# A graph network's edge loop on one core: counts moved ahead of the later sources, spans read at the body's head, ranks restarted behind each block's loop

## The reference, cut to what matters

```python
# layer 0: a two-layer message network, summed over the edges of each source
m = jnp.concatenate([x[row], x[col]], axis=1)
m = jax.nn.relu(m @ Wm1 + bm1)
m = jax.nn.relu(m @ Wm2 + bm2)
m_sum = jax.ops.segment_sum(m, row, num_segments=x.shape[0])

# layer 2: each source keeps only its first 10 edges, by rank in the list
rank = jnp.arange(E) - starts[row_s]
keep = (rank < NUM_NEIGHBORS).astype(x.dtype)

# layer 3: edge weights, summed over equal (source, target)
msg = edge_weight[:, None] * x[src]
agg = jax.ops.segment_sum(msg, dst, num_segments=N)
```

## Time and profile before

| what | value |
|---|---|
| median of three executions | 982.04 us (979.52 to 982.39) |
| profiled execution, span | 979.5 us; the page gives no other time of its own, and it lies at the lowest of the three |
| PE busy | 888.5 us, 91% of the span |
| DVE busy | 665.4 us, 68% |
| ACT busy | 502.9 us, 51% |
| POOL busy | 292.3 us, 30% |
| chain that ended last | PE 76%, DVE 13%, ACT 5%, issue 3% |
| mean granted clock of PE | 0.986 of full speed |

### The profile page before, as it was taken

The page is one execution under the profiler, slowest core; times in us unless marked ns, Lnnn a source line. Parts: engine busy times, 40 slices in busy tenths (PEclk is TensorE's granted clock), DMA queues, the critical chain, the costliest instruction groups (busy, mean ns, idle before and its releaser), DMA issues.

```text
span 979.5 us, 18566 instructions
## 1 busy us (share of the span) xinstructions
PE 888.5 (91%) x5440; PEld 549.7 (56%) x5474; DVE 665.4 (68%) x1778; ACT 502.9 (51%) x1009; POOL 292.3 (30%) x424
## 2 busy tenths in 40 slices
PE   3999968999899989999999989889998998899898
PEld 1556736878787878787887855522233222322244
DVE  6399995676667666667666674676858776877561
ACT  6232103555555555565555563746755665566621
POOL 5030027444444545455444510021132210112000
PEclk9999987999999999999999999999999999999999
DMA  3020022111111111112111200000000000000120
GB/s 82 19 91 1 1 78 97 52 54 53 60 49 65 44 64 43 65 48 70 37 64 41 51 33 1 1 0 1 1 1 1 0 1 1 0 1 1 69 104 22
DMA packets 19145, 35.87 MB, mean 37 GB/s; under 512 B 5280, under 2 KB 11552, under 8 KB 18976
## 3 DMA queue, kind: packets, MB, share of 16 engines
q0 software_dynamic: 7104, 19.41, 6.7%
q1 hardware_dynamic: 12000, 15.95, 4.6%
HBM read 29.56 MB, written 5.79 MB: 36 GB/s over the span
## 4 chain that ended last, share of the span: by engine, by line
PE 76%; DVE 13%; ACT 5%; issue 3%; DMA 1%; POOL 1%; DVEq 0%; ACTq 0%; POOLq 0%
PE PS L1396 9%; PE PS L1258 7%; PE PS L1252 6%; PE PS L1381 5%; PE PS L1177 5%; PE PS L1178 5%; PE PS L1192 5%; PE PS L1127 5%; PE PS L1387 4%; PE PS L1249 3%; PE PS L1299 3%; DVE OHd L988 3%; PE PS L1170 3%; PE PS L1350 2%; PE PS L1183 2%
## 5 line engine op out<-in xcount | busy, mean ns | idle before, releaser
L399 POOL DMA_INDIRECT BT<-Qtab,gidx x148 | 150.4, 1016 | 96.3 <-DVE gidx L815 61.1
L546 ACT ACTIVATE OHe<-OHs,sew 128x128 bf16<-128x128 bf16 x408 | 126.6, 389 | 61.9 <-PE PS L1258 61.4
L413 POOL TENSOR_SCALAR KV<-BT,pid 128x256 bf16<-128x256 uint8 x74 | 69.9, 945 | 174.2 <-DVE MS L890 168.1
L988 DVE CUSTOM_DVE_ANT_0 OHd<-PS,n1T 128x1024 bf16<-128x1024 f32 x96 | 112.1, 1219 | 9.5 <-PE PS L1350 9.5
L557 ACT ACTIVATE m2s<-m2s 128x512 f32<-128x512 f32 x68 | 42.9, 630 | 107.9 <-DVE m2s L916 107.9
L930 DVE TENSOR_SCALAR OHd<-iotaN,dstf 128x1024 bf16<-128x1024 f16 x136 | 63.6, 507 | 37.0 <-PE PS L1258 37.0
L916 DVE TENSOR_TENSOR m2s<-PS,bm 128x512 f32<-128x512 f32 x68 | 46.9, 690 | 53.9 <-PE PS L1178 53.9
L1177 PE MATMUL PS<-Wm,m1T 128*128 128x256 f32 x276 | 83.2, 383 | 0.0
L1178 PE MATMUL PS<-Wm,m1T 128*128 128x256 f32 x276 | 82.6, 381 | 0.0
L1258 PE MATMUL PS<-OHs,m2s 128*128 128x128 f32 x544 | 79.5, 290 | 0.1
L452 POOL TENSOR_TENSOR zl<-AL,Sx 128x8 f32<-128x8 f32 x12 | 2.6, 216 | 257.0 <-DVE Sx L988 257.0
(11 more groups left out here) (350 smaller groups left out, 1723.9 us busy)
## 6 DMA issues: line engine op xcount, KB each, us to landing
BT<-Wtab SPq DMA_DIRECT2D x1, 4096.0 KB, 13.9
BT<-Qtab,gidx POOLq DMA_INDIRECT x148, 2.8
BT<-Stab SPq DMA_DIRECT2D x1, 2048.0 KB, 10.5
Wtab<-H SPq DMA_DIRECT2D x4, 512.0 KB, 2.9
Wtab<-cs SPq DMA_DIRECT2D x4, 512.0 KB, 3.0
Qtab<-BT SPq DMA_DIRECT2D x1, 1024.0 KB, 4.5
Wn<-in_L_gnn_Wn SPq DMA_DIRECT2D x1, 1024.0 KB, 5.4
x<-in_x SPq DMA_DIRECT2D x1, 512.0 KB, 4.1
```

Source lines behind the costliest of these rows:

```text
L399: g.indirect_dma_start(out=G[:, p % SLOTS, k, :], out_offset=None, in_=Qtab, in_offset=bass.IndirectOffsetOnAxis(ap=gidx[:, p, k:k + 1], a ...
L546: a.activation(OHe[:, k, j, :], OHs[:, k, :], ACT.Copy, scale=sew[:, j, bass.ds(2 * g + k, 1)])
L988: v.tensor_tensor_reduce(junk[n % 2], bank(4, 2), mask[:, i, :], 1.0, 2 * FAR, ALU.subtract, ALU.max, Sx[:, i, hd:hd + 1]).then_inc(S("gat ...
```

## The change

PE's body is put in another order: the span is read at the head, before R'; C follows R'; and S follows C. The semaphore `counts_added` is now raised by S's first product, where M's first product raised it before. On DVE the source one-hots `OHs` come ahead of the message. At a block's end ACT copies the message sums ahead of the weights; PE restarts the ranks as soon as the message sums are out, the restart clearing bank 4 itself, and then clears banks 0 to 3 only. Behind the last block neither is done.

```diff
@@ ScalarE, at a block's end
                 eng.wait_ge(S("ranks_done"), end + 1)
+                a.activation(msum[:, :, b * P:(b + 1) * P], bank(4)[:, 0:F2].rearrange("p (f n) -> p f n", f=2),
+                             ACT.Copy)\
+                    .then_inc(S("msum_out"), 1)
                 if b >= 2:
                     eng.wait_ge(S(f"spilled{b % 2}"), 16 * (b // 2))
                 a.activation(TT[b % 2], bank(2, 2), ACT.Copy).then_inc(S("weights_out"), 1)
-                a.activation(msum[:, :, b * P:(b + 1) * P], ...
@@ VectorE, in the body
-                    message(g + 2)
-
                     eng.wait_ge(S("ranks_added"), g + 1)
                     eng.wait_ge(S("scaled_ready"), g + 1)
                     eng.wait_ge(S("counts_ready"), g + 1)
...
                     last.then_inc(S("src_onehots"), 1)
+                    message(g + 2)
                     eng.wait_ge(S("counts_added"), g + 2)
@@ TensorE
-            def ranks(pairs):
+            def ranks(pairs, anew=False):
-                for region, tri, k in pairs:
+                for i, (region, tri, k) in enumerate(pairs):
                     last = t.matmul(bank(4)[:, F2 + region * P:F2 + (region + 1) * P], tri[:], OHs[:, k, :],
-                                    start=False, stop=False, skip_group_check=True)
+                                    start=anew and i == 0, stop=False, skip_group_check=True)
                 return last
+            def restarted():
+                ranks(((0, beforeb, 0), (1, onesb, 0), (1, beforeb, 1)), anew=True).then_inc(S("ranks_restarted"), 1)
-            def sources(slot, blk):
+            def sources(slot, blk, behind=None):
                 for k in range(2):
                     for j in range(3):
+                        if behind is not None and k == 0 and j == 1:
+                            last.then_inc(behind, 1)
                         last = t.matmul(bank(5)[:, k * F2:(k + 1) * F2],
...
-            for b in range(NB):
-                eng.wait_ge(S("src_onehots"), g0 + 1)
-                ranks(((0, beforeb, 0), (1, onesb, 0), (1, beforeb, 1))).then_inc(S("ranks_restarted"), 1)
+            eng.wait_ge(S("src_onehots"), 1)
+            restarted()
+            for b in range(NB):
                 with eng.Fori(g0, end) as g:
+                    eng.wait_ge(S("spans"), 1)
+                    span = eng.value_load(rngi[0:1, bass.ds(g, 1)], min_val=1, max_val=NB * NB * NB - 1)
+                    first, least, past = eng.snap((span >> 6) & (NB - 1)), eng.snap((span >> 3) & 7), eng.snap((span & 7) + 1)
                     eng.wait_ge(S("ranks_read"), g + 1)
                     ranks(((0, notbefb, 0), (0, onesb, 1), (1, notbefb, 1))).then_inc(S("ranks_added"), 1)
-                    eng.wait_ge(S("spans"), 1)
-                    span = eng.value_load(rngi[0:1, bass.ds(g, 1)], min_val=1, max_val=NB * NB * NB - 1)
-
-                    eng.wait_ge(S("turned_onehots"), g + 3)
-                    sources((g + 2) & (SLOTS - 1), (span >> 6) & (NB - 1))
 
                     eng.wait_ge(S("scaled_ready"), g + 1)
                     eng.wait_ge(S("counts_ready"), g + 1)
-                    with eng.Fori((span >> 3) & 7, (span & 7) + 1, 2) as d:
+                    with eng.Fori(least, past, 2) as d:
...
+                    eng.wait_ge(S("turned_onehots"), g + 3)
+                    sources((g + 2) & (SLOTS - 1), first, S("counts_added"))
+
                     eng.wait_ge(S("m2_ready"), g + 1)
...
-                            if f == 0 and k == 0:
-                                last.then_inc(S("counts_added"), 1)
                     last.then_inc(S("pair_done"), 1)
@@ TensorE, at a block's end
+                eng.wait_ge(S("msum_out"), b + 1)
+                if b + 1 < NB:
+                    restarted()
+                eng.wait_ge(S("weights_out"), b + 1)
                 eng.wait_ge(S("counts_out"), b + 1)
-                eng.wait_ge(S("msum_out"), b + 1)
-                for k in range(5):
-                    t.matmul(bank(k), zeros[:, 0:P], zeros[:, 0:BANK], start=True, stop=True)
+                if b + 1 < NB:
+                    for k in range(4):
+                        t.matmul(bank(k), zeros[:, 0:P], zeros[:, 0:BANK], start=True, stop=True)
```

More of the change, by code:

```diff
@@ L566, in _ @@
                 a.activation(TT[b % 2], bank(2, 2), ACT.Copy).then_inc(S("weights_out"), 1)
-                a.activation(msum[:, :, b * P:(b + 1) * P], bank(4)[:, 0:F2].rearrange("p (f n) -> p f n", f=2),
-                             ACT.Copy)\
-                    .then_inc(S("msum_out"), 1)
                 g0, end = end, after
```

## The result

The changed kernel takes 1036.3 us (four runs, 1034.47 to 1036.87) against 982.2 us before: ratio 1.0554, 95% interval 1.0538 to 1.057. The forecast was 1024 with a range of 1003 to 1034. The direction was right, the size 12 us short and 2 us outside the range. The profiled execution has a span of 1032.7 us against 979.5, so 53.2 us more, where the sum of the prediction had 43.7.

The account below looks back on a forecast made before the run. A loop through DVE and PE's sequencer was to bound each pair: 60 pairs x 0.64 = 38.4, seven block ends 4.7, one more pair 0.6, together 43.7 us on 982.0, 1025.7, put 2 lower at 1024; range 1003 to 1034.

Parts of the forecast that it names:

- S's steps behind C: Inside a pair on PE: S's six address steps stand uncovered behind C's loop, 0.62 us, making C to S 1.74 us.
- DVE's ring: Inside a pair: S, message, `OHd`, `prod`, `OHc`, C, next S; 6.14 us, taken as 6.12, 0.64 more a pair.
- `OHd` to `prod` 301.44 - 300.59 = 0.85: On DVE inside a pair: time from the start of `OHd` to `prod`, put at 0.85 us.
- The other five terms: S to message 1.18, message to next operation 0.61, `prod` to `OHc` end 1.16, on to C 0.60, to S 1.74 us.
- steps hidden by C: On PE behind C: S's steps may be partly hidden by C's last products, so the forecast was put 2 us lower.
- The second ring through the transposes: Inside a pair: L's transposes wait for the message about 0.1 us more, which was said to lie within the DVE loop.
- The block ends: At seven block ends: 9.80 us against 9.13, 0.67 more each, although 1.04 us of exposed span reading goes.
- the clock as a rival: With PE idle in each pair the granted clock might fall oftener; ten pairs at about 1.3 us, 1037 us; chance 0.04.
- Inside a block it was covered before and still is, by L: nothing: Inside a block, moving the span's reading to the head was said to change nothing, since L covers it either way.
- The sequencer hides it (960): C's products are queued far ahead, so S's steps pass beside C and 0.22 us a pair goes; 960 us, chance 0.09.
- PE alone (1009): PE's own steps set the pair at 5.88 us, 0.40 more, the DVE loop being shorter; 1009 us, chance 0.10.
- the cancelling case (981): S's steps are hidden by half and block ends gain 1.04 us, so gains and loss cancel; 981 us, chance 0.05.

Follow-up runs that it names:

- Experiment 2: The changed kernel with five of S's six address steps done at the body's head and kept in registers; 1009.7 us, 1.0208 of the kernel before.
- Experiment 3: The changed kernel with GpSimd's one-hots held back until the counting one-hots `OHc` are there; 1038.2 us, 1.0504 of the kernel before.
- experiment 6: The changed kernel with the four clearing products at a block's end done three times over; 1032.7 us, 1.0461 of the kernel before.
- experiment 9: The changed kernel with the span read behind R' again, before C's set-up; 1045.1 us, 1.0572 of the kernel before.
- experiment 4: The kernel before with only the span's reading moved to the head of PE's body, ahead of R'; 947.9 us, 0.9591.
- experiments 1: The changed kernel with S ahead of C again: with DVE's order as before 952.5 us, 0.9636; with DVE's new order 947.8 us, 0.961.
- experiment 10: The changed kernel with S's address steps kept in registers and GpSimd's one-hots held back, together; 1067.4 us, 1.0794 of the kernel before.
- experiment 8: A second span reading added: in the kernel before, between R' and S, 1035.0 us, 1.0475; with the reading at the head, there, 968.2 us, 0.9781.

## Why the prediction was right in kind and short in size

*S's steps behind C: right.* 1.74 us from C to S, as worked out. Experiment 2 took five steps away and the distance fell by 0.48. The sequencer's records of L1197 in one pair of the changed kernel:

```profile
L1197 PEldq FUSED_REGOPS  x5: 46/46/65, 228.7 to 229.3; - x5
L1197 PEldq ALU_OP  x3: 32/36/36, 228.5 to 228.8; - x3
```

They last 0.03 to 0.05 us each and begin at 228.5, with S at 228.99. Start to start is what counts, 0.6 us and not 0.2. The Trainium skill (Perfetto Trace Analysis, Per-engine timelines) says that for an instruction of the sequencer only the execution is reported, and the runs agree.

*DVE's ring sets the pair: right, with one term too small.* This is the step that failed: "`OHd` to `prod` 301.44 - 300.59 = 0.85". It measures 1.02. The other five terms are within 0.01. The 0.85 was read where only the last 0.25 us of GpSimd's one-hot lay beside `OHd`:

```profile
299.90 0.94 POOL L413 TENSOR_SCALAR KV<-BT,pid 128x256 bf16<-128x256 uint8 x1 [2.07 <-DVE MS L890]
```

In the changed kernel `OHd` follows the message at once, and so does GpSimd's one-hot, which waits for that same message. The two kernels' lines over the whole trace (ns min/median/max), first of before:

```profile
L930 DVE TENSOR_SCALAR OHd<-iotaN,dstf x136: 467/485/658, 163.3 to 563.7; 128x1024 bf16<-128x1024 f16 x136
...
L413 POOL TENSOR_SCALAR KV<-BT,pid x74: 910/945/962, 145.7 to 562.5; 128x256 bf16<-128x256 uint8 x74
```

and of after:

```profile
L929 DVE TENSOR_SCALAR OHd<-iotaN,dstf x136: 475/589/704, 162.8 to 618.2; 128x1024 bf16<-128x1024 f16 x136
...
L413 POOL TENSOR_SCALAR KV<-BT,pid x74: 912/1163/1167, 144.5 to 618.0; 128x256 bf16<-128x256 uint8 x74
```

0.17 us by the 60 distances inside blocks is 10.2 us. The misses against the sum are 8.3 us inside blocks (46.7 for 38.4), 3.0 at the block ends (7.7 for 4.7) and 1.7 the other way around them, together about the 9.5 between 53.2 and 43.7; the forecast of 1024 had taken 2 more off for steps hidden by C, which were not hidden. The inside is 8.3 and not 10.2 because pairs above the median one added 7.0 us before (335.8 less 60 x 5.48) and 5.1 after.

Of the two instructions of `OHd` the second is the long one, 0.70 us; the first, with GpSimd's beside it for its last 0.30 us, kept its 0.48. Experiment 3 shows the cause: apart, the two engines' instructions take 0.48 and 0.93. That it returned 0.05 a pair and not 0.17 says nothing against the term, since S's products ended 0.20 later there. The second ring through the transposes, which the prediction had put at "about 0.1 us more", is about 0.13 us shorter than the first in the changed kernel: C stands 0.30 us behind R' there in the median, and 0.17 in experiment 3, where it waits for nothing else.

The Trainium skill (SBUF — State Buffer, Who interferes with whom) names such a pair: a DVE `tensor_scalar` can run in modes that take two ports, one of them shared with GpSimd, and whichever instruction comes first keeps the shared ports to its end while the other is fully blocked. The profile does not name `OHd`'s mode. That they disturb each other agrees; the full blocking does not, as far as the recorded ends on GpSimd can be trusted. GpSimd's instruction ends at 230.95 + 1.16 = 232.11, and blocked until then, DVE's second one-hot would have put `prod` behind 232.11, where it starts at 231.79. The prediction had not weighed this rule.

*The block ends: right without the clock.* The two ends with no fall of the clock take 9.86 and 9.89 us, forecast 9.80. The five with one take 10.4 to 10.9, and the pair behind each about 0.3 more. The end with 10.9 is longer by itself: it takes 9.67 in the kernel before, and 10.35 in experiment 6 with no fall. The prediction had the clock as a rival at 0.04 ("I give it little"), priced at 13 us; it came true beside the forecast and not in place of it, with about 4.9 us by experiment 6. That the rival's 1037 is nearest to the 1036.3 measured is luck. The mistake was to make it a rival: it adds to whichever case holds.

*"Inside a block it was covered before and still is, by L: nothing": wrong.* In the changed kernel it is nearly right (0.12 us a pair, experiment 9). In the kernel before, moving it is the largest gain of any single edit tried here: 0.41 us a pair and 1.27 at each end, 4.1% (experiment 4). I had asked whether the array waits at the reading. The question was what the reading delays behind it: 0.87 from S to C and 1.12 from C to M in the earlier trace rows each held 0.22 us of sequencer time. The prediction had seen the first of them, and put it to C's own set-up. So the change holds a gain of 4% that needs S ahead of C, and a swap that undoes it; the swap costs about 6.29 - 5.14 = 1.15 us a pair, not the 0.64 that the difference to before shows.

*The sequencer hides it (960): wrong in this kernel.* Its 960 is near what experiments 1 and 4 took, 0.959 to 0.964 of the kernel before, but by another cause: the place of the reading, and with S ahead of C. The Trainium skill (TensorE: Matmul & The Clock Gate, the table at its head) gives TensorE's queue a depth of 64. The runs show no lead of that size: one more reading of 0.65 us in a body of 48 products costs 0.34 us at the head and all of 0.65 three products later.

*PE alone (1009) and the cancelling case (981): did not happen.* C stands 0.30 to 0.35 us behind R' and not 0.17, and the pair is the ring's 6.29 and not PE's 5.88.

*What was to show it:* 6.1 us a pair, found 6.29; about 0.5 us of "issue" before S some 68 times, found 0.55; C 0.6 us behind `OHc`, found 0.60; no wait before `OHd` and no 1.04 at the ends, found so. A pair whose counts loop turns twice takes 7.70 us, 1.41 more than the others, as in the earlier trace rows.

## What to carry to other kernels

A loop body that reads or computes its addresses on the engine's own sequencer has two lines to keep short, the array's and the sequencer's: put such steps where long static work lies behind them, and ask of each not whether something waits at it but what it delays next. Before a step is moved behind a wait, count the dynamic steps that will stand in the open there, start to start. When a duration is carried into a new order, look at what will run beside it then: the 0.85 us was read where GpSimd's one-hot had all but ended. And an edit that holds one engine back moves all that stands behind it in that engine's stream, as the gathers were moved in experiments 3 and 10.

## What the runs showed of the hardware

- `OHd`'s one-hot on DVE and GpSimd's slow each other when they overlap, and by the records neither waits for the other's end: 0.48 to 0.70 us on DVE, 0.93 to 1.16 on GpSimd.
- A reading of one value into a register on PE's sequencer is recorded as 0.30 us and costs 0.65 in a body that the sequencer sets (experiment 8).
- Whether a reading is free depends on a few products: three of them earlier it gave 0.41 us a pair.
- The semaphore of a PE product can rise well behind the end that the profile models for the product: 1.08 us in experiment 10 and 0.20 in experiment 3, each time with a GpSimd gather issued beside it; without one it was 0.01 in all 613 turns. The cause is not shown.
